# Attention of a two-layer kernel: four PSUM banks for scores and three for maxima, maxima ordered beside scores of the other half, heads written out

## The chip, the core and the metric

One core of a Trainium2 chip runs the whole program. The metric is the time of one execution on the device in microseconds; lower is better. Three runs of the kernel before give the median that the change is measured against.

## What is computed

Two layers, each a gated cross-attention and a gated mixture-of-experts feed-forward on x of 2048 x 256. The keys and values of both layers come from the same context of 1601 x 256. There are 16 heads of depth 16. The change touches the attention alone:

```python
q = split(layernorm(x) @ wq.T + bq); k = split(ctx @ wk.T + bk); v = split(ctx @ wv.T + bv)
scores = einsum('bhqd,bhkd->bhqk', q, k) / sqrt(16)
scores = where(mask == 0, -inf, scores)          # layer 0 only
p = softmax(scores); x = x + tanh(g) * (einsum('bhqk,bhkd->bhqd', p, v) @ wo.T + bo)
# routed feed-forwards follow each attention: one expert of 8 in layer 0, two of 8 in layer 1
```

Layer 0's mask leaves keys only in a stretch at the end of the context. If they fit a window of 512 keys, which they do here, `attend` runs over that window (4 key tiles); layer 1 runs over all 1601 keys (13 key tiles, the last of 65 keys).

## The kernel before

`attend` (L589 on) computes all 16 heads of one layer. TensorE, ScalarE and VectorE each have an instruction list of their own, written in the order in which they are to run, tied by counting semaphores (`wait`). An engine stands at a wait until its semaphore is high enough, and all that is behind in its list stands too.

Each head needs two passes over its scores. The first finds the maxima of the rows: TensorE computes scores with queries as rows (`entry`, L798: one *piece* is 128 queries x 400 keys, 16 x 4 = 64 pieces a head in layer 1; 128 x 512, 16 pieces, in layer 0) and VectorE reduces each to a column (`piece`, L910). When all are done VectorE reduces again to `row_max` (L944), TensorE transposes it (`maxima`, L787), VectorE splits it into two parts (`split_max`, L916, L918), and a DMA puts them into rows of the queries' operand. The second pass computes scores with keys as rows (`scores`, L809: 128 keys x 512 queries, four *columns* S0 to S3 a key tile), less the maximum by those rows; ScalarE takes the exponential into `probs` (L890), and `times_values` (PV, L826) multiplies with the values, four matmuls side by side into one bank, `o_bank`. A further column of ones gives the sums. After the last key tile ScalarE copies `o_bank` out (`copy_out`, L873), TensorE transposes it (`sums`, L791), and VectorE takes the reciprocal and multiplies (`norm`, L926, L929).

The two passes are interleaved: iteration i makes the maxima of head i, and the exponentials and products of heads i-1 and i-2. An iteration has KT *steps* (13 in layer 1, 4 in layer 0), and each step takes its share of pieces (`cuts`): five in twelve steps of layer 1 and four in the first; four in each step of layer 0. A step s < `late` (4, or 2 in layer 0) works at the last key tiles of head i-2, the others at head i-1. The transpose of the maxima stands in step 1 of layer 1 (step 0 of layer 0) as the third entry; the sums stand at the end of step 6 (3). Both count as two entries. Iterations 16 and 17 only drain: they have no pieces.

TensorE's list in a step with pieces p0 to p4 is: S0, S1, p0, p1, S2, p2, PV, S3, p3, p4. PV is for the key tile of the step before. The scores of even columns and the pieces of even number use rows 0 to 63 of the array, the others rows 64 to 127; two matmuls on different halves can run side by side.

Banks and waits: the scores go round three banks of PSUM, and a score waits for the exponential of the third score before it. The entries (pieces, transposes) go round four banks (`BANKS`), and entry n waits for VectorE to be done with entry n-4 (`entry_done`). `o_bank` takes the eighth bank. PV waits for all four exponentials of its key tile.

The iterations run through `iterations`: 0 to 3 are written out, 4 to 15 are a loop in the engines' instructions whose body has three iterations (so three jumps back), 16 and 17 are written out. In the loop, waits compare with values held in registers. SP, which issues the loads of the next head's keys and queries, has a loop of its own.

Of the kernel before, what the change touches and what calls it, by code (L numbers as in the profile page):

```python
# [22 lines left out]
F32 = mybir.dt.float32  # L23
# [3 lines left out]
ALU = mybir.AluOpType  # L27
ACT = mybir.ActivationFunctionType
# [23 lines left out]
BANKS = 4  # L52
# [327 lines left out]
class Keys:  # L380


    def __init__(self, first, size, pieces, late, maxima_at):
        self.first, self.S, self.pieces = first, size, pieces
        self.KT = -(-size // P)
        self.late = late
        self.maxima_at = maxima_at
        self.sums_at = min(late + 2, self.KT - 1)
        assert sum(n for _, n in pieces) == size and (NC * self.KT) % RING == 1
# [199 lines left out]
def attend(nc, const, scratch, l, keys, attn, row_max, mask=None, key_mask=None):  # L589
# [9 lines left out]
    with ExitStack() as ctx:  # L599
# [12 lines left out]
        s_bank = [sc.ps(f"s_bank{n}", [P, CH], F32) for n in range(RING)]  # L612
# [27 lines left out]
        assert ENTRIES % BANKS == 0 and (NC * KT) % RING == 1  # L640

        def entries(mx, tail, fresh):


            steps, n = [], 0
            for s in range(KT):
                now = list(range(cuts[s], cuts[s + 1])) if mx else []
                if fresh and s == keys.maxima_at[0]:
                    now.insert(keys.maxima_at[1] if mx else 0, "maxima")
                now += ["sums"] * (s == keys.sums_at and tail)  # L650
                steps.append([])
                for what in now:
                    n += places(what)
                    steps[-1].append((what, n - 1))
            return steps, n
# [20 lines left out]
        def bank_of(i, n):  # L676
            return p_bank[((entries_before(i) if isinstance(i, int) else -6) + n) % BANKS]

# [4 lines left out]
        def iterations(eng, body):  # L683

            def once(i):
                body(i, i % RING, i < H, i >= 2, 1 <= i <= H)
            for i in range(4):
                once(i)
            with eng.Fori(4, H - RING + 1, RING) as j:
                for u in range(RING):  # L690
                    body(j + u, (4 + u) % RING, True, True, True)
            for i in range(H, H + 2):
                once(i)
# [14 lines left out]
        def _(sp):  # L708
# [43 lines left out]
            with sp.Fori(4, H - RING, RING) as j:  # L752
                for u in range(RING):
                    body(j + u, (4 + u) % RING, True, True, True)
            for i in range(H - RING, H + 1):
                body(i, i % RING, True, True, True)
# [21 lines left out]
        def _(pe):  # L778
# [3 lines left out]
            def entry(i, slot, what, n):  # L782
                wait(pe, entry_done, entries_before(i) + (n - BANKS + 1))
                bank = bank_of(i, n)
                if what == "maxima":
                    wait(pe, max_ready, i)
                    last = pe.transpose(bank[0:QT, 0:P], row_max[:, (slot - 1) % RING, :], const["ident"][:, :])  # L787
                elif what == "sums":
                    wait(pe, o_copied, i - 1)
                    for b in range(NC):  # L790
                        last = pe.transpose(bank[:, b * P:(b + 1) * P], o_sb[:, b * P:(b + 1) * P],  # L791
                                            const["ident"][:, :])
                else:
                    t, c = tile_of(what)
                    k0, kn = PIECES[c]
                    a, t = divmod(t, QT // 2)
                    rows = slice(a * SIDE, a * SIDE + ROWS)
                    last = pe.matmul(bank[:, 0:even(kn)], q_st[rows, slot, t * P:(t + 1) * P].bitcast(F32R),  # L798
                                     k_st[rows, slot, k0:k0 + even(kn)].bitcast(F32R), start=True, stop=True)
                last.then_inc(entry_ready, places(what))  # L800

            def scores(h, hs, kt, c):
                kn, q0 = keys_of(kt), chunk_of(c)
                if not isinstance(h, int) or NC * (KT * h + kt) + c >= RING:
                    wait(pe, exp_done, h * (NC * KT) + (NC * kt + c - RING + 1), apart=masked)
                out = s_bank[(NC * kt + c + hs) % RING][0:kn, :]
# [24 lines left out]
            def body(i, slot, mx, tail, fresh):  # L831
# [6 lines left out]
                for s in range(KT):  # L838
# [3 lines left out]
                    for chunks, first, end in (((0, 1), 0, 2), ((2,), 2, 3), ((3,), 3, None)):  # L842
# [10 lines left out]
        def _(act):  # L853
# [21 lines left out]
            def body(i, slot, mx, tail, fresh):  # L875
                for s in range(KT):
# [3 lines left out]
                    if now:  # L880
# [4 lines left out]
                        for c in range(NC):  # L885
                            if c == NC - 1 and s == LATE and tail:
# [4 lines left out]
                                           s_bank[(NC * kt + c + hs) % RING][0:kn, :], ACT.Exp).then_inc(exp_done, 1)  # L891
# [4 lines left out]
        def _(dve):  # L896
# [3 lines left out]
            def piece(i, slot, what, n):  # L900
# [4 lines left out]
                if masked:  # L905
                    dve.tensor_tensor_reduce(junk[:, n % BANKS, 0:kn], bank_of(i, n)[:, 0:kn],
                                             mask[:, t, k0:k0 + kn], 1.0, -3.0e38, ALU.add, ALU.max, dst)\
                        .then_inc(entry_done, 1)
                else:
                    dve.tensor_reduce(dst, bank_of(i, n)[:, 0:kn], AX.X, ALU.max).then_inc(entry_done, 1)  # L910

            def split_max(i, n):

                wait(dve, entry_ready, entries_before(i) + (n + 1))
                turned = bank_of(i, n)[0:QT, 0:P]
# [6 lines left out]
            def norm(i, slot, n):  # L922

                wait(dve, entry_ready, entries_before(i) + (n + 1))
                sums = bank_of(i, n)[:, :].rearrange("p (b c v) -> p b c v", b=NC, v=VW)
# [6 lines left out]
            def body(i, slot, mx, tail, fresh):  # L932
                listed, many = entries(mx, tail, fresh)
                for step in listed:
                    for what, n in step:
                        if what == "maxima":
                            split_max(i, n)
# [882 lines left out]
def flamingo_kernel(nc, io, out):  # L1820
# [10 lines left out]
    with ExitStack() as ctx:  # L1831
# [16 lines left out]
        everything = Keys(0, S, PIECES, 4, (1, 2))  # L1848
        for l in range(2):
            if l:  # L1850
                clear_semaphores(nc)
            with ExitStack() as part:
# [17 lines left out]
                else:  # L1870
                    attend(nc, const, scratch, l, everything, attn, row_max)
# [48 lines left out]
```

## Time and profile before

| | |
|---|---|
| median of 3 runs | 1890.03 us (1886.89 to 1894.4) |
| profiled execution | 1891.61 us, its span 1889.9 us |
| mean granted TensorE clock | 0.901 |
| PE busy | 1545.9 us (82%) |
| DVE busy | 1178.3 us (62%) |
| ACT busy | 861.1 us (46%) |
| POOL busy | 182.0 us (10%) |
| attention of layer 0 | first piece at 169.7 us, last norm at 385.5 us |
| attention of layer 1 | last norm at 1585.5 us; row maxima of its heads from 967.0 to 1537.2 us |

PE is TensorE's matmuls, DVE VectorE, ACT ScalarE, POOL GpSimd, SP the engine that issues DMAs. A row of a timeline has the start in us from the span's start, the time that it covers, the engine, the line of the kernel, what is written and read, and how many instructions were merged (x3). In square brackets stands how long the engine had been idle and what ended that. The ends of matmuls are modelled, and some records can be missing, so starts are the better numbers. In the table of windows the columns are: from and to, length, busy time (and count) of PE, PE's weight loads, DVE, ACT and POOL, then TensorE's granted clock as a share of full speed, the DMA engines' busy share and GB/s. The windows of rows 2 run from one row maximum (L944) to a later one, that is over whole heads: one head, three heads, three single heads, 13 heads of layer 0, and a part of the drain.

### The profile page before, as it was taken

The page shows a single profiled execution, that of the slowest core. Times are in us where ns is not written, and L with a number is a line of the kernel's source. Part 1 is how long each engine was busy: PE and PEld are TensorE (multiplying, and loading weights), DVE is VectorE, ACT ScalarE, POOL GpSimd, SP SyncE. Part 2 cuts the span into 40 slices and gives each one's busy share as a digit, 9 for nine tenths or more (in the row PEclk, how much of TensorE's full clock was granted, in tenths as well). Part 3 has the DMA queues.
Part 4 walks back from the last instruction along what each step waited for, and adds up shares of the span by engine and source line. Part 5 has one row for each costly group of instructions (what it writes and reads, how often), then busy time and mean ns, then how long its engine had stood idle before and what let it go on. Part 6 is the DMA issues. An engine that isn't in the chain of part 4 may idle for free. (4 is left out here: it accounts for less than half of the span.)

```text
span 1889.9 us, 27747 instructions
## 1 busy us (share of the span) xinstructions
PE 1545.9 (82%) x7833; PEld 910.5 (48%) x7834; DVE 1178.3 (62%) x2309; ACT 861.1 (46%) x1544; POOL 182.0 (10%) x248
## 2 busy tenths in 40 slices
PE   6464999968997999992399999999999998657880
PEld 3132443347785788882154444444444434544550
DVE  2564988763211677766398888888898853622334
ACT  3021767722112555541127777676776775221110
POOL 3520000000300000003000000000000000061106
PEclk9786999987999999996659999999999999788995
DMA  7935312111102899971722121111211100424114
GB/s 242 373 116 156 102 43 51 27 46 67 45 1 88 300 348 336 335 250 48 212 67 67 42 44 23 22 22 30 35 22 22 22 1 1 113 89 129 38 50 133
DMA packets 108654, 196.61 MB, mean 104 GB/s; under 512 B 8958, under 2 KB 80371, under 8 KB 108567
## 3 DMA queue, kind: packets, MB, share of 16 engines
q1 hardware_dynamic: 101633, 180.71, 30.9%
q0 software_dynamic: 4608, 12.59, 2.1%
q10 hardware_dynamic: 2326, 2.31, 0.4%
q8 instruction: 36, 0.59, 0.1%
q14 instruction: 51, 0.42, 0.1%
HBM read 144.69 MB, written 50.36 MB: 103 GB/s over the span
## 5 line engine op out<-in xcount | busy, mean ns | idle before, releaser
L910 DVE TENSOR_REDUCE attend_piece_max<-attend_p_bank 128x1 f32<-128x400 f32 (+3 forms) x1280 | 671.8, 588 | 108.1 <-PE attend_p_bank L798 90.7
L890 ACT ACTIVATE attend_probs<-attend_s_bank 128x512 f32<-128x512 f32 (+1 forms) x1088 | 565.3, 602 | 284.4 <-PE attend_s_bank L809 284.2
L798 PE MATMUL attend_p_bank<-attend_k_st,attend_q_st 62*128 62x400 f32 (+2 forms) x1280 | 412.3, 418 | 62.8 <-DMA attend_k_st<-ones_rows 52.3
L809 PE MATMUL attend_s_bank<-attend_q_st,attend_k_st 64*128 64x512 f32 (+1 forms) x1088 | 385.5, 461 | 26.8 <-ACT attend_probs L890 13.6
L809 PEld LDWEIGHTS attend_s_bank<-attend_q_st,attend_k_st 64*128 64x128 f32 (+1 forms) x1088 | 170.9, 185 | 348.9 <-ACT attend_probs L890 338.0
L826 PE MATMUL attend_o_bank<-attend_probs,attend_v_st 128*32 128x512 f32 (+1 forms) x2176 | 293.4, 611 | 1.4 <-ACT attend_probs L890 1.4
L798 PEld LDWEIGHTS attend_p_bank<-attend_k_st,attend_q_st 62*128 62x128 f32 x1280 | 223.1, 198 | 109.5 <-issue 54.0
L1520 DVE TENSOR_TENSOR slots_w_low<-slots_w_up,slots_w_high 128x2048 fp32r<-128x2048 f32 x46 | 105.1, 2287 | 46.9 <-ACT slots_w_high L1516 46.9
L1330 DVE TENSOR_TENSOR share_hid<-share_b_bank,share_g_act 128x512 f32<-128x512 f32 (+1 forms) x40 | 27.6, 691 | 120.5 <-PE share_b_bank L1181 89.8
L1516 ACT ACTIVATE slots_w_high<-slots_w_up 128x2048 fp32r<-128x2048 f32 x46 | 87.8, 1910 | 6.8 <-DMA slots_w_up<-in_L_ffn_W_dram 6.6
L1787 POOL DMA_INDIRECT collect_back<-back,keep_f_place x48 | 47.0, 980 | 386.4 <-PEq L1776 372.4
L1476 PE MATMUL slots_y_bank<-slots_w_dn,slots_hid_t 128*128 128x256 f32 x368 | 83.2, 379 | 1.0 <-DVE slots_hid_t L1527 1.0
L773 POOL COPY attend_v_st<-attend_values 128x64 f32 (+3 forms) x32 | 9.3, 298 | 735.7 <-PE attend_o_bank L826 706.5
L1148 POOL DMA_INDIRECT sorted<-keep_x_x_n,keep_f_place x48 | 48.3, 1005 | 324.9 <-DVE keep_f_place L1313 310.9
L1757 DVE TENSOR_TENSOR slots_hid<-slots_u_bank,slots_g_act 128x192 f32<-128x192 f32 x39 | 13.9, 358 | 101.9 <-ACT slots_g_act L1743 101.9
L826 PEld LDWEIGHTS attend_o_bank<-attend_probs,attend_v_st 128*32 128x32 f32 (+1 forms) x2176 | 42.9, 108 | 69.8 <-ACT attend_probs L890 47.9
L1193 PE MATMUL share_y_bank<-share_w_dn,share_hid 128*128 128x256 f32 (+1 forms) x320 | 71.2, 382 | 6.1 <-DVE share_hid L1330 6.1
L1690 PE MATMUL slots_u_bank<-keep_f_up,slots_x_t 128*128 x156 | 63.3, 530 | 14.8 <-issue 12.9
L1476 PEld LDWEIGHTS slots_y_bank<-slots_w_dn,slots_hid_t 128*128 128x128 f32 x368 | 69.7, 190 | 11.3 <-issue 1.2
L1193 PEld LDWEIGHTS share_y_bank<-share_w_dn,share_hid 128*128 128x128 f32 (+1 forms) x320 | 60.0, 190 | 17.1 <-DVE share_hid L1330 9.1
L1218 ACT ACTIVATE share_g_act<-share_a_bank 128x512 f32<-128x512 f32 (+1 forms) x40 | 23.9, 598 | 83.5 <-PE share_a_bank L1181 72.2
L1743 ACT ACTIVATE slots_g_act<-slots_u_bank 128x192 f32<-128x192 f32 x39 | 12.9, 330 | 102.0 <-PE slots_u_bank L1690 102.0
(234 smaller groups left out, 1811.0 us busy)
## 6 DMA issues: line engine op xcount, KB each, us to landing
slots_w_up<-in_L_ffn_W_dram SPq DMA_DIRECT2D x46, 1024.0 KB, 7.9
slots_w_dn<-in_L_ffn_W_dram SPq DMA_DIRECT2D x23, 1024.0 KB, 6.1
ctx_raw<-in_mask_BxSxS_ik_dram SPq DMA_DIRECT2D x16, 800.5 KB, 8.1
q_rows<-q_part SPq DMA_DIRECT2D x24, 512.0 KB, 4.3
attend_q_st<-q_rows SPq DMA_DIRECT2D x64, 192.0 KB, 4.6
k_rows<-ctx_k_part SPq DMA_DIRECT2D x12, 800.5 KB, 10.5
attend_k_st<-k_rows SPq DMA_DIRECT2D x32, 300.2 KB, 6.1
sorted<-keep_zeros SPq DMA_DIRECT2D x6, 1024.0 KB, 8.5
```

Of the source, the lines that this page charges most:

```text
L798: last = pe.matmul(bank[:, 0:even(kn)], q_st[rows, slot, t * P:(t + 1) * P].bitcast(F32R), k_st[rows, slot, k0:k0 + even(kn)].bitcast(F32R ...
L809: last = pe.matmul(out, k_st[rows, hs, kt * P:kt * P + kn].bitcast(F32R), q_st[rows, hs, q0:q0 + CH].bitcast(F32R), start=True, stop=not m ...
L826: last = pe.matmul(o_bank[c * VW:(c + 1) * VW, :], v_st[0:kn, hs, kt, :], probs[0:kn, (kt + hs) % RING, c * CH:(c + 1) * CH], start=(kt == ...
L890: act.activation(probs[0:kn, (kt + hs) % RING, q0:q0 + CH], s_bank[(NC * kt + c + hs) % RING][0:kn, :], ACT.Exp).then_inc(exp_done, 1)
L910: dve.tensor_reduce(dst, bank_of(i, n)[:, 0:kn], AX.X, ALU.max).then_inc(entry_done, 1)
L1148: pool.indirect_dma_start(scratch["sorted"][l][:, :], bass.IndirectOffsetOnAxis(ap=place[:, k, t:t + 1], axis=0), x_n[:, t], None).then_in ...
L1193: last = pe.matmul(y_bank[n % 2][:, :], hid[:, c % 2, f, t * P:(t + 1) * P], w_dn[:, f], start=(f == 0), stop=(f == FT - 1))
L1476: last = pe.matmul(y_bank[:, 0:D], hid_t[:, slot, f], w_dn[:, slot, f], start=(f == 0), stop=(f == FT - 1))
L1516: act.activation(w_high[:, half].bitcast(F32R), loaded(slot, half), ACT.Copy).then_inc(w_rounded, 1)
L1520: dve.tensor_tensor(w_low[:, half].bitcast(F32R), loaded(slot, half), w_high[:, half], ALU.subtract)\
L1690: last = pe.matmul(u_bank[k][:, 0:2 * F], x_t[:, k, b], resident["up"][:, e, b].rearrange("p a n f -> p (a n f)"), start=(b == 0), stop=(b ...
L1787: pool.indirect_dma_start(back[:, k, t], None, scratch["back"][l][:, :], bass.IndirectOffsetOnAxis(ap=place[:, k, t:t + 1], axis=0))\
```

## The change

1. Four score banks (one for each column), three banks for entries. A score now waits for the exponential of the same column of the key tile before; entry n waits for entry n-3. As 68 entries a head don't divide by three, the bank depends on the iteration's slot.
2. `side_by_side` reorders the pieces of a step, so that the first is of the other half than S0, the second of the other half than S1, and so on. TensorE's list becomes S0, p0, S1, p1, S2, p2, PV, S3, p3, p4.
3. With `looped=False` all heads are written out, without a loop in the instructions, on each engine. Layer 1 and layer 0's window run so; only the branch of layer 0 that isn't taken here keeps the loop.

```diff
-BANKS = 4
+BANKS = 3
...
-        s_bank = [sc.ps(f"s_bank{n}", [P, CH], F32) for n in range(RING)]
+        s_bank = [sc.ps(f"s_bank{n}", [P, CH], F32) for n in range(NC)]
         p_bank = [sc.ps(f"p_bank{n}", [P, CH], F32) for n in range(BANKS)]
...
+        def side_by_side(now):
+
+            halves, taken = [now[1::2], now[0::2]] if now and now[0] % 2 == 0 else [now[0::2], now[1::2]], []
+            for k in range(len(now)):
+                taken.append((halves[k % 2] or halves[1 - k % 2]).pop(0))
+            return taken
...
-                now = list(range(cuts[s], cuts[s + 1])) if mx else []
+                now = side_by_side(list(range(cuts[s], cuts[s + 1]))) if mx else []
...
-        def bank_of(i, n):
-            return p_bank[((entries_before(i) if isinstance(i, int) else -6) + n) % BANKS]
+        def bank_of(i, slot, n):
+            return p_bank[((entries_before(i) if isinstance(i, int) else slot * ENTRIES - 6) + n) % BANKS]
...
-            for i in range(4):
+            for i in range(4 if keys.looped else H):
                 once(i)
-            with eng.Fori(4, H - RING + 1, RING) as j:
-                for u in range(RING):
-                    body(j + u, (4 + u) % RING, True, True, True)
+            if keys.looped:
+                with eng.Fori(4, H - RING + 1, RING) as j:
+                    for u in range(RING):
+                        body(j + u, (4 + u) % RING, True, True, True)
...
-            with sp.Fori(4, H - RING, RING) as j:
-                for u in range(RING):
-                    body(j + u, (4 + u) % RING, True, True, True)
-            for i in range(H - RING, H + 1):
+            if keys.looped:
+                with sp.Fori(4, H - RING, RING) as j:
+                    for u in range(RING):
+                        body(j + u, (4 + u) % RING, True, True, True)
+            for i in range(H - RING if keys.looped else 4, H + 1):
                 body(i, i % RING, True, True, True)
...
             def scores(h, hs, kt, c):
                 kn, q0 = keys_of(kt), chunk_of(c)
-                if not isinstance(h, int) or NC * (KT * h + kt) + c >= RING:
-                    wait(pe, exp_done, h * (NC * KT) + (NC * kt + c - RING + 1), apart=masked)
-                out = s_bank[(NC * kt + c + hs) % RING][0:kn, :]
+                if not isinstance(h, int) or KT * h + kt > 0:
+                    wait(pe, exp_done, h * (NC * KT) + (NC * kt + c - NC + 1), apart=masked)
+                out = s_bank[c][0:kn, :]
...
-                    for chunks, first, end in (((0, 1), 0, 2), ((2,), 2, 3), ((3,), 3, None)):
+                    for chunks, first, end in (((0,), 0, 1), ((1,), 1, 2), ((2,), 2, 3), ((3,), 3, None)):
                         if chunks == (3,) and before:
                             times_values(*before)
...
-        everything = Keys(0, S, PIECES, 4, (1, 2))
+        everything = Keys(0, S, PIECES, 4, (1, 2), looped=True)
+        unmasked = Keys(0, S, PIECES, 4, (1, 2))
...
-                    attend(nc, const, scratch, l, everything, attn, row_max)
+                    attend(nc, const, scratch, l, unmasked, attn, row_max)
```

## Rows read from the trace of the kernel before

**Rows 1.** Page, costliest groups: busy us, mean ns, idle before, releaser.

```profile
L910 DVE TENSOR_REDUCE attend_piece_max<-attend_p_bank 128x1 f32<-128x400 f32 (+3 forms) x1280 | 671.8, 588 | 108.1 <-PE attend_p_bank L798 90.7
```

**Rows 2.** Windows: length, busy us and count by engine, clock, DMA.

```profile
1040.14:1077.69 37.55, 35.86 (x227) 15.73 (x225) 33.26 (x70) 27.50 (x54) 0.36 (x1) 1.00 0.24 53
...
1077.69:1189.64 111.95, 107.71 (x677) 47.40 (x675) 99.97 (x207) 82.19 (x160) 1.08 (x3) 1.00 0.17 29
...
1189.64:1230.43 40.79, 37.37 (x227) 16.71 (x225) 33.27 (x69) 27.66 (x54) 0.36 (x1) 0.96 0.14 26
...
1305.12:1347.06 41.94, 38.61 (x227) 17.35 (x225) 33.27 (x70) 27.73 (x54) 0.36 (x1) 0.92 0.14 25
...
1421.71:1462.53 40.82, 37.34 (x227) 16.68 (x225) 33.27 (x69) 27.64 (x54) 0.36 (x1) 0.96 0.15 26
...
203.46:366.21 162.75, 155.40 (x895) 65.29 (x894) 144.82 (x273) 115.24 (x222) 2.84 (x12) 1.00 0.19 45
...
1556.94:1577.74 20.80, 17.19 (x97) 5.09 (x96) 0.00 (x0) 16.52 (x34) 0.00 (x0) 1.00 0.00 1
```

**Rows 3.** Timeline of TensorE, a step of layer 1: start, us, instruction.

```profile
1135.56 0.45 PE L798 MATMUL attend_p_bank<-attend_k_st,attend_q_st 62*128 62x400 f32 x1 [0.21 <-DVE keep_a_attn L929]
...
1135.93 1.07 PE L826 MATMUL attend_o_bank<-attend_probs,attend_v_st 128*32 128x512 f32 x8
...
1136.93 0.49 PE L809 MATMUL attend_s_bank<-attend_q_st,attend_k_st 64*128 64x512 f32 x1
...
1138.11 0.50 PE L809 MATMUL attend_s_bank<-attend_q_st,attend_k_st 64*128 64x512 f32 x1
...
1138.28 0.44 PE L798 MATMUL attend_p_bank<-attend_k_st,attend_q_st 62*128 62x402 f32 x1
...
1138.65 0.64 PE L826 MATMUL attend_o_bank<-attend_probs,attend_v_st 128*32 128x512 f32 x4
```

**Rows 4.** The same stretch, VectorE.

```profile
1135.08 0.42 DVE L929 TENSOR_TENSOR keep_a_attn<-attend_p_bank,attend_inv_sum 128x256 f32 x1 [0.20 <-DVE attend_inv_sum L926]
...
1135.42 1.52 DVE L910 TENSOR_REDUCE attend_piece_max<-attend_p_bank 128x1 f32<-128x400 f32 x3
...
1137.65 1.53 DVE L910 TENSOR_REDUCE attend_piece_max<-attend_p_bank 128x1 f32<-128x400 f32 x3 [0.70 <-PE attend_p_bank L798]
```

**Rows 5.** The same stretch, ScalarE.

```profile
1137.46 2.06 ACT L890 ACTIVATE attend_probs<-attend_s_bank 128x512 f32<-128x512 f32 x4 [1.07 <-PE attend_s_bank L809]
```

**Rows 6.** Timeline around the maxima's transpose, layer 1.

```profile
1117.76 0.28 PE L787 MATMUL attend_p_bank<-keep_ident,keep_a_row_max 128*16 128x128 f32 x1
...
1117.96 1.06 PE L826 MATMUL attend_o_bank<-attend_probs,attend_v_st 128*32 128x512 f32 x8
...
1118.96 0.50 PE L809 MATMUL attend_s_bank<-attend_q_st,attend_k_st 64*128 64x512 f32 x1
...
1119.53 2.50 DVE L910 TENSOR_REDUCE attend_piece_max<-attend_p_bank 128x1 f32<-128x399 f32 x5 [0.56 <-PE attend_p_bank L798]
...
1121.01 1.06 PE L826 MATMUL attend_o_bank<-attend_probs,attend_v_st 128*32 128x512 f32 x8
```

**Rows 7.** Timeline of layer 1's drain, where no maxima are made.

```profile
1562.14 1.06 PE L826 MATMUL attend_o_bank<-attend_probs,attend_v_st 128*32 128x512 f32 x8
...
1563.14 0.73 PE L809 MATMUL attend_s_bank<-attend_q_st,attend_k_st 64*128 64x512 f32 x3
...
1563.67 1.57 ACT L890 ACTIVATE attend_probs<-attend_s_bank 128x512 f32<-128x512 f32 x3 [0.54 <-PE attend_s_bank L809]
...
1564.32 0.49 PE L809 MATMUL attend_s_bank<-attend_q_st,attend_k_st 64*128 64x512 f32 x1 [0.45 <-ACT attend_probs L890]
...
1564.74 0.64 PE L826 MATMUL attend_o_bank<-attend_probs,attend_v_st 128*32 128x512 f32 x4
```

**Rows 8.** Timeline of TensorE in layer 1's fill, low clock.

```profile
979.53 1.93 PE L826 MATMUL attend_o_bank<-attend_probs,attend_v_st 128*32 128x512 f32 x8
...
983.82 0.64 PE L826 MATMUL attend_o_bank<-attend_probs,attend_v_st 128*32 128x512 f32 x4
```

More of the change, by code:

```diff
@@ L380, with __init__ @@
 class Keys:
-    def __init__(self, first, size, pieces, late, maxima_at):
+    def __init__(self, first, size, pieces, late, maxima_at, looped=False):
+        self.looped = looped
         self.first, self.S, self.pieces = first, size, pieces
@@ L639, in attend @@
         ENTRIES = PER + 4
-        assert ENTRIES % BANKS == 0 and (NC * KT) % RING == 1
+        assert (NC * KT) % RING == 1 and BANKS == RING
+        def side_by_side(now):
[3 more added lines that the diff above has]
+            return taken
         def entries(mx, tail, fresh):
@@ L783, in entry @@
                 wait(pe, entry_done, entries_before(i) + (n - BANKS + 1))
-                bank = bank_of(i, n)
+                bank = bank_of(i, slot, n)
                 if what == "maxima":
@@ L890, in body @@
                             act.activation(probs[0:kn, (kt + hs) % RING, q0:q0 + CH],
-                                           s_bank[(NC * kt + c + hs) % RING][0:kn, :], ACT.Exp).then_inc(exp_done, 1)
+                                           s_bank[c][0:kn, :], ACT.Exp).then_inc(exp_done, 1)
             iterations(act, body)
@@ L905, in piece @@
                 if masked:
-                    dve.tensor_tensor_reduce(junk[:, n % BANKS, 0:kn], bank_of(i, n)[:, 0:kn],
+                    dve.tensor_tensor_reduce(junk[:, n % BANKS, 0:kn], bank_of(i, slot, n)[:, 0:kn],
                                              mask[:, t, k0:k0 + kn], 1.0, -3.0e38, ALU.add, ALU.max, dst)\
@@ L909, in piece, with split_max @@
                 else:
-                    dve.tensor_reduce(dst, bank_of(i, n)[:, 0:kn], AX.X, ALU.max).then_inc(entry_done, 1)
-            def split_max(i, n):
+                    dve.tensor_reduce(dst, bank_of(i, slot, n)[:, 0:kn], AX.X, ALU.max).then_inc(entry_done, 1)
+            def split_max(i, slot, n):
                 wait(dve, entry_ready, entries_before(i) + (n + 1))
-                turned = bank_of(i, n)[0:QT, 0:P]
+                turned = bank_of(i, slot, n)[0:QT, 0:P]
                 dve.tensor_scalar(m_part[:, 0].bitcast(F32R), turned, -1.0, None, ALU.mult).then_inc(max_high, 1)
@@ L924, in norm @@
                 wait(dve, entry_ready, entries_before(i) + (n + 1))
-                sums = bank_of(i, n)[:, :].rearrange("p (b c v) -> p b c v", b=NC, v=VW)
+                sums = bank_of(i, slot, n)[:, :].rearrange("p (b c v) -> p b c v", b=NC, v=VW)
                 dve.reciprocal(inv_sum[:, slot], sums[:, :, :, DK]).then_inc(inverted, 1)
@@ L936, in body @@
                         if what == "maxima":
-                            split_max(i, n)
+                            split_max(i, slot, n)
                         elif what == "sums":
```

## The prediction

> **What bounds the kernel now.** I read the costliest groups of the page first. The costliest one, the maxima's reductions on VectorE (L910, 671.8 us), lies in the two attention stages [rows 1], and so does the change. The windows then show two things. A head of layer 1 takes 111.95 / 3 = 37.32 us (the time from one head's row maximum to the next), of which VectorE works 99.97 / 3 = 33.3 us; a head of layer 0 takes 162.75 / 13 = 12.52 us with 144.82 / 13 = 11.14 us of VectorE [rows 2]. So VectorE is nearest to being full, yet idle 11% of each head. And in layer 1 three heads take 40.79, 41.94 and 40.82 us instead of 37.32: each holds a jump back of the hand-written loop over three heads [rows 2].
>
> The timeline says why VectorE idles. A step is one tile of 128 keys: four score matmuls S0 to S3, five maxima matmuls p0 to p4 and PV, the values matmul. In one step PV starts at 1138.65, after S at 1138.11 and p at 1138.28; the step before, PV starts at 1135.93 and S3 at 1136.93 behind it [rows 3]. ScalarE's four exponentials start at 1137.46 [rows 5], 0.53 after S3. S2 of the next step wants the bank of this first exponential (three score banks), so it starts at 1138.11. That makes a ring: S3, 0.53, exponential 0.60, release 0.05, S2 to PV 0.54, PV to S3 1.00, together 2.72 us, the distance 1135.93 to 1138.65 exactly [rows 3, 5]. (Where p2 uses the same half of the array as S2, it can't run beside it, and the ring is about 0.07 longer; steps alternate between 2.72 and 2.79, mean 2.76.) The drain, where no maxima are made, shows the ring bare: S3 1563.14, exponential 1563.67, S2 1564.32, PV 1564.74, against PV 1562.14 before: 2.60 us [rows 7]. VectorE needs only 5 x 0.48 = 2.4 us in a step (three reductions in 1.52, the last 0.56 long [rows 4]), and then waits for the p behind PV (0.70 us in the row shown, after the sums [rows 4]; in a regular step 2.76 - 4 x 0.48 - 0.56 = 0.26 on average).
>
> **Four score banks.** S2 now needs the exponential of its own column in the step before, which is long past. PV still needs the exponential that follows S3. Without maxima the ring is 0.53 + 0.60 + 0.05 + 1.00 = 2.18 instead of 2.60: 0.42 less [rows 7]. Some 15 such steps in layer 1's drain and 5 in layer 0's give -6.3 and -2.1 us.
>
> **Three maxima banks.** Entry n waits for the reduction of n-3, not n-4, and TensorE takes its instructions in order. The entry just ahead of PV is p2. In a five-piece step the entries before it are p1, p0, and then p4 of the step before. So p2, and PV queued behind it, now wait until p4 has been reduced; with four banks it was p3, one reduction earlier. How this reads on the trace: VectorE ends norm at 1135.08 + 0.42 = 1135.50, the p that waits for it starts at 1135.56, PV at 1135.93, S3 at 1136.93 [rows 3, 4]. So: release 0.06, lone p to PV 0.37, PV to S3 1.00. From an S3 with its p beside it to the reduction it takes 0.57 (1118.96 to 1119.53 [rows 6]); where p shares the half it is 0.72 (1136.93 to 1137.65 [rows 3, 4]). The new ring is: p3's reduction starts 0.57 after S3, p4's 0.48 later, it takes 0.56, release 0.06, p2 to PV 0.37, PV to S3 1.00: 3.04 us against 2.76, +0.28 a step. Low bound: if PV followed p2 by 0.30 (0.17 of its columns and little else) 2.97; and if p4 were reduced where it is now relative to ScalarE, no less than 2.72. High bound: p3 not beside S3, 0.15 more, 3.19. I take 3.04, since each piece has a row.
>
> **The order of maxima.** p0 to p3 get the other half from S0 to S3. That keeps p3 at 0.57 in every step (now in every second), and is in the 3.04 already; it also makes S2 and p2 cheap, but S2 is no longer on the path, so this is worth nothing. In the step with the maxima transpose the order slips by one: the p behind S3 falls on S3's half, 0.15 later.
>
> **One head of layer 1.** Ten of 13 steps are rings of 3.04: +2.8 us. The transpose's step: it waits for p0 (one reduction after p3) and PV is 0.20 behind it (1117.76 to 1117.96 [rows 6]): 1.57 + 0.48 + 0.56 + 0.06 + 0.20 = 2.87, +0.1. The step after: 1.00 + 0.72 + 2 x 0.48 + 0.99 = 3.67, where 1121.01 - 1117.96 = 3.05 stands now [rows 6], +0.6. The step after the sums: they take two places in the ring of banks, so p1 and p2 both wait for norm, where now only p2 does: +0.20 for p1, +0.17 since p2 no longer stands alone, and the transposes start one release later, about +0.35: +0.7. Head: 37.3 + 4.2 = 41.5. For the 14 full heads +58.4; the first head with scores has eight or so such steps, +2.2.
>
> **One head of layer 0** has four steps of four pieces of 512 columns, and this p2 waits for p3 of the step before: 0.61 + 0.68 + 0.06 + 0.40 + 1.00 = 2.75 (an estimate: the terms above with 112 more columns, 0.04 of TensorE and 0.12 of VectorE). Two steps are such. The one after the transpose has p2 on S3's half and two reductions behind it: 1.00 + 0.76 + 0.61 + 0.68 + 0.06 + 0.40 = 3.5. In the step after the sums norm starts some 2.7 after PV, p0's reduction 0.57 behind it, and the transpose waits for that one: 2.7 + 0.57 + 0.68 + 0.06 + 0.20 = 4.2. Head 2 x 2.75 + 3.5 + 4.2 = 13.2 against 12.52, 14 heads: +9.5.
>
> **Heads written out.** The three jumps back cost 3.5 + 4.6 + 3.5 = 11.6 us of layer 1, with TensorE's clock down to 0.92 to 0.96 in those heads; they go [rows 2]. Layer 0's heads differ by 0.1 at most with a jump: -0.4. What the longer code costs: heads 2 and 3 are written out already, and one of them takes 37.55 against 37.32 [rows 2]. Bounds: between nothing and 0.23 x 12 = 2.8; I take nothing, for its DMA share is also the higher (0.24 against 0.17: the zeros being stored). Each engine, SP with its loads too, keeps its order; register arithmetic for waits leaves the sequencers and is on no path, since the rings above close without it. On the cause the Trainium skill has a rule (Runtime: NRT & Kernel Launch, "Instruction fetch mechanics"): a taken branch whose target is out of the fetch window waits for a fetch, straight code is fetched ahead. By that rule the 11.6 us go whole, and the trace agrees on the jumps' place.
>
> **Sum**, against the profiled execution's own 1891.6: layer 1 +58.4 + 2.2 - 11.6 - 6.3; layer 0 +9.5 - 0.4 - 2.1: +49.7, 1941.3. The median of the three runs is 1.6 lower than the profiled one: 1939.7.
>
> **Rivals.**
> - *The gate of p2 holds less than I say* (slower by half): p4 reduced earlier, or PV closer to p2, ring 2.90, half of the attention's +70: 1905. It is inside my range. For it: the ring has six terms of 0.05 to 1.0, each modelled in the records.
> - *Steps keep 2.76* because p4's reduction never ends after the exponential: only jumps and drain count, 1890.0 - 20.4 = 1870. Against it: p3's reduction starts 0.57 after S3 and the exponential 0.53, both 0.6 long; p4's ends 0.5 later. Chance 0.06.
> - *VectorE becomes the bound and full*, what the fourth score bank could give with maxima banks to spare: heads 33.3 and 11.1, 14 x 4.0 + 14 x 1.4 = 76 less, and 20 more: 1794. Against it: with three banks VectorE has 3 x 0.48 = 1.45 us of stock from p2's start, and PV, S3 and p3 take 0.37 + 1.00 + 0.57 = 1.94. Chance 0.06.
> - *TensorE's clock falls.* The new step holds some 0.5 us in which TensorE waits for p2. At the low level a step took 983.82 - 979.53 = 4.29 us [rows 8]; if half the steps of the 14 heads ran so, 91 x 1.2 = 109 more: 2049. Against it: the drain waits in every 2.60 us step (S2 at 1564.32 behind a wait [rows 7]) and the full level is granted there: 1.00 from 1556.94 to 1577.74 [rows 2]. Chance 0.04. The Trainium skill's page TensorE: Matmul & The Clock Gate ("A second HAM failure mode: psum-queue depth-cycling") speaks for this rival: short idles between groups that cycle PSUM banks made another kernel's clock oscillate. The row of the drain doesn't show it.
>
> **How the numbers follow.** Forecast and the half case together 0.84: nearly all of it more than 0.5% (9.5 us) above 1890, which is what a measurement of this kernel can tell from no change. Faster 0.12 by the second and third rival, same 0.03, slower 0.85. The range runs from the half case, 1905, to the unpaired ring (0.15 x 13 x 14 = 27, of which I take 20): 1960. It leaves out the two faster rivals and the clock, 0.16, and a little of the rest.
>
> **What would show it.** Right: row maxima of layer 1 some 41.5 us apart, of layer 0 13.2; PV to PV 3.04 in a regular step; the p ahead of PV released by L910 of VectorE and starting 0.06 after a reduction's end; VectorE's idle time before p3 near 3.04 - 4 x 0.48 - 0.56 = 0.54 us instead of 0.26; no head of 41 to 42 among heads of another length; PV to PV 2.2 in the drain. Wrong: PV released by L890, or PV to PV at or under 2.76 in layer 1; a clock under 1.00 in the regular heads would be the last rival.

## The result, and the profile after

The changed kernel takes 1937.84 us (median of 4 runs, 1935.05 to 1940.19) against 1888.85 for the kernel before beside it: 1.025 times, 95% interval 1.021 to 1.029. Forecast were 1939.7 and 1905 to 1960. The profiled execution spans 1938.5 us, 48.6 more than before. (Here and below, the ratios and intervals leave out a run at a markedly lower clock and over 1.5% above the kernel's fastest, one of e2's four; the medians hold all runs.)

On the page, the idle time ahead of the reductions has grown (162.8 us; 108.1 in rows 1), and so has that of TensorE's weight loads (PEld) ahead of the maxima, most of it ended by VectorE. The third line is the one of before:

```profile
L920 DVE TENSOR_REDUCE attend_piece_max<-attend_p_bank 128x1 f32<-128x400 f32 (+3 forms) x1280 | 674.6, 591 | 162.8 <-PE attend_p_bank L808 161.7
...
L808 PEld LDWEIGHTS attend_p_bank<-attend_k_st,attend_q_st 62*128 62x128 f32 x1280 | 211.3, 195 | 257.3 <-DVE attend_piece_max L920 183.7
...
L798 PEld LDWEIGHTS attend_p_bank<-attend_k_st,attend_q_st 62*128 62x128 f32 x1280 | 223.1, 198 | 109.5 <-issue 54.0
```

The windows of the changed kernel, with the columns of rows 2: 14 full heads of layer 1, a regular head of it, two heads that were longer, 13 heads of layer 0, and a part of the drain.

```profile
1008.71:1591.78 583.07, 529.99 (x3156) 225.20 (x3156) 469.12 (x966) 387.26 (x743) 4.68 (x13) 0.99 0.15 29
...
1050.09:1091.48 41.39, 37.62 (x226) 15.99 (x225) 33.51 (x69) 27.64 (x54) 0.36 (x1) 1.00 0.22 48
...
1257.04:1299.79 42.75, 38.98 (x226) 16.50 (x225) 33.51 (x69) 27.74 (x54) 0.36 (x1) 0.96 0.14 25
...
1465.33:1508.99 43.66, 40.10 (x227) 17.04 (x225) 33.48 (x69) 27.92 (x54) 0.36 (x1) 0.92 0.14 25
...
194.70:364.50 169.80, 160.43 (x895) 64.71 (x895) 145.08 (x273) 117.91 (x222) 3.07 (x13) 1.00 0.22 54
...
1604.90:1626.70 21.80, 19.36 (x122) 6.19 (x120) 0.42 (x1) 20.45 (x41) 0.00 (x0) 1.00 0.00 1
```

A regular head of layer 1 takes 41.39 us where rows 2 have 37.32, one of layer 0 169.80 / 13 = 13.06 where they have 12.52. VectorE works in a head what it did (33.51 and 33.3): it only waits longer. Two heads have 42.75 and 43.66: they hold no jump; TensorE's clock fell to the low level in them (mean 0.96 and 0.92), both times in the step behind PV of the tile of 65 keys, 2.2 to 2.3 us after that PV started. In the step where it fell, the next PV covers 1.93 us instead of 1.06:

```profile
1273.38 1.93 PE L836 MATMUL attend_o_bank<-attend_probs,attend_v_st 128*32 128x512 f32 x8
```

```profile
1481.70 1.93 PE L836 MATMUL attend_o_bank<-attend_probs,attend_v_st 128*32 128x512 f32 x8
```

One regular step of TensorE, VectorE and ScalarE, to be laid beside rows 3 to 5. Of the scores, the first of these lines is S3 and the second S2 of the next step; of the maxima, p1 and p2 are shown:

```profile
1200.79 1.06 PE L836 MATMUL attend_o_bank<-attend_probs,attend_v_st 128*32 128x512 f32 x8
...
1201.79 0.50 PE L819 MATMUL attend_s_bank<-attend_q_st,attend_k_st 64*128 64x512 f32 x1
...
1202.50 0.39 PE L819 MATMUL attend_s_bank<-attend_q_st,attend_k_st 64*128 64x512 f32 x1
...
1202.99 0.45 PE L808 MATMUL attend_p_bank<-attend_k_st,attend_q_st 62*128 62x400 f32 x1
...
1203.47 0.45 PE L808 MATMUL attend_p_bank<-attend_k_st,attend_q_st 62*128 62x400 f32 x1
...
1203.84 1.06 PE L836 MATMUL attend_o_bank<-attend_probs,attend_v_st 128*32 128x512 f32 x8
```

```profile
1202.36 2.50 DVE L920 TENSOR_REDUCE attend_piece_max<-attend_p_bank 128x1 f32<-128x400 f32 x5 [0.55 <-PE attend_p_bank L808]
```

```profile
1202.32 2.06 ACT L900 ACTIVATE attend_probs<-attend_s_bank 128x512 f32<-128x512 f32 x4 [0.98 <-PE attend_s_bank L819]
```

PV starts at 1200.79, S3 at 1201.79 and the next PV at 1203.84, so the step takes 3.05 us. The exponential of S3 (1202.32 to 1202.92) has ended 0.92 before PV starts, so it holds nobody. p1 and p2 come at 1202.99 and 1203.47. The reductions start at 1202.36 and then each 0.48 later, and the last is 0.56 long. So the one of p3 ends at about 1202.92 and the one of p4 at 1203.41: each p starts 0.06 to 0.07 behind one. PV follows p2 by 0.37. VectorE idles 0.55 before p3's reduction. The waits of the weight loads over the 14 heads say the same, the changed kernel first:

```profile
PEld attend_s_bank L819 <- ACT attend_probs L900: 151.5, 180, 1.4
...
PEld attend_p_bank L808 <- DVE attend_piece_max L920: 124.2, 318, 0.9
```

```profile
PEld attend_s_bank L809 <- ACT attend_probs L890: 223.2, 343, 0.8
...
PEld attend_p_bank L798 <- DVE attend_piece_max L910: 18.0, 45, 2.1
```

The wait for the exponentials has shrunk from 223 to 152 us, and the wait for the reductions has grown from 18 us in 45 places to 124 us in 318. In the drain PV follows PV by 2.18 us (2.60 in rows 7):

```profile
1609.28 1.07 PE L836 MATMUL attend_o_bank<-attend_probs,attend_v_st 128*32 128x512 f32 x8 [0.22 <-ACT attend_probs L900]
...
1611.46 1.07 PE L836 MATMUL attend_o_bank<-attend_probs,attend_v_st 128*32 128x512 f32 x8 [0.22 <-ACT attend_probs L900]
...
1613.64 0.64 PE L836 MATMUL attend_o_bank<-attend_probs,attend_v_st 128*32 128x512 f32 x4 [0.22 <-ACT attend_probs L900]
```

### The profile page after: what moved, and what is told of

It reads as the page before. It is cut to its first block and busy times, and to the rows that moved or that the text cites. A ratio compares the mean times of both kernels' runs of the same rounds, so it can differ in the third digit from the quotient of the medians.

```text
span 1938.5 us, 23827 instructions
## 1 busy us (share of the span) xinstructions
PE 1569.8 (81%) x7833; PEld 911.9 (47%) x7834; DVE 1182.4 (61%) x2309; ACT 866.9 (45%) x1544; POOL 183.1 (9%) x248
## 5 line engine op out<-in xcount | busy, mean ns | idle before, releaser
L920 DVE TENSOR_REDUCE attend_piece_max<-attend_p_bank 128x1 f32<-128x400 f32 (+3 forms) x1280 | 674.6, 591 | 162.8 <-PE attend_p_bank L808 161.7
L900 ACT ACTIVATE attend_probs<-attend_s_bank 128x512 f32<-128x512 f32 (+1 forms) x1088 | 571.7, 601 | 327.1 <-PE attend_s_bank L819 324.0
L808 PE MATMUL attend_p_bank<-attend_k_st,attend_q_st 62*128 62x400 f32 (+2 forms) x1280 | 459.8, 446 | 97.5 <-DMA attend_k_st<-ones_rows 50.2
L819 PE MATMUL attend_s_bank<-attend_q_st,attend_k_st 64*128 64x512 f32 (+1 forms) x1088 | 375.2, 429 | 0.0
L808 PEld LDWEIGHTS attend_p_bank<-attend_k_st,attend_q_st 62*128 62x128 f32 x1280 | 211.3, 195 | 257.3 <-DVE attend_piece_max L920 183.7
L783 POOL COPY attend_v_st<-attend_values 128x64 f32<-128x64 f32 (+1 forms) x32 | 9.3, 298 | 788.0 <-PE attend_o_bank L836 760.9
L1158 POOL DMA_INDIRECT sorted<-keep_x_x_n,keep_f_place x48 | 48.5, 1011 | 320.6 <-DVE keep_f_place L1323 306.6
```

The source lines that it names most:

```text
L819: last = pe.matmul(out, k_st[rows, hs, kt * P:kt * P + kn].bitcast(F32R), q_st[rows, hs, q0:q0 + CH].bitcast(F32R), start=True, stop=not m ...
L900: act.activation(probs[0:kn, (kt + hs) % RING, q0:q0 + CH], s_bank[c][0:kn, :], ACT.Exp).then_inc(exp_done, 1)
L920: dve.tensor_reduce(dst, bank_of(i, slot, n)[:, 0:kn], AX.X, ALU.max).then_inc(entry_done, 1)
L1158: pool.indirect_dma_start(scratch["sorted"][l][:, :], bass.IndirectOffsetOnAxis(ap=place[:, k, t:t + 1], axis=0), x_n[:, t], None).then_in ...
```

## The experiments

Two theories stand against each other in most of them. The *gate*: the entry ahead of PV waits for the reduction as many entries back as there are banks, PV is queued behind it, and VectorE runs dry while PV holds TensorE. The *rivals*: the written-out code, the new order, or the fourth score bank is what costs. Lengths of steps are distances from PV to PV in the traces. The diffs are cut to what matters ("...").

**Loops put back (e1_looped).**

```diff
-        unmasked = Keys(0, S, PIECES, 4, (1, 2))
+        unmasked = Keys(0, S, PIECES, 4, (1, 2), looped=True)
...
-        keys = Keys(start, WINDOW, [(0, WINDOW)], 2, (0, 2))
+        keys = Keys(start, WINDOW, [(0, WINDOW)], 2, (0, 2), looped=True)
```

> The changed kernel with the loop over three heads put back in both layers; banks and order as changed. Gate theory (p2 waits for the reduction three entries back, PV is queued behind it): PV to PV stays at 3.05 us in a regular step, the three jumps back return in layer 1 with 11.6 us: 1938 + 11 = 1949. Rival (written-out code is what costs): the regular step falls under 2.9 and the time under 1925.

Measured: 1960.2 us, 1.036 times the kernel before (1.028 to 1.043). Regular steps keep 3.05 us, so the written-out code isn't what costs. But the loop costs 22 us here, not 11: the 14 heads take 605.33 us at a mean clock of 0.96, where they take 583.07 at 0.99 written out. The heads with a jump have 48.5, 47.8 and 47.8 us at clocks of 0.86 to 0.89. The step with the jump is about 2.7 us longer than the same step elsewhere (2.5 in the kernel before); most of the rest is the low clock. Three heads without a jump hold a fall of the clock too.

```profile
1015.25:1620.58 605.33, 547.48 (x3156) 233.11 (x3156) 469.05 (x966) 388.69 (x744) 4.69 (x13) 0.96 0.14 28
```

**Before, written out (e2_written).** Only `Fori` is dropped from the kernel before, as in the change.

> The kernel before with its heads written out, nothing else. Gate theory: the regular steps stay at 2.72 and 2.79 us, the heads of 41 to 42 us go: 1889 - 12 = 1877. Rival (written-out code costs): 1889 or more.

Measured: 1871.64 us, 0.989 (0.979 to 0.998); one of the four runs took 1900.24 at a mean clock of 0.88. No head is longer than 37.2. The 14 heads take 520.16 us against 534.20:

```profile
995.94:1516.10 520.16, 501.72 (x3153) 219.70 (x3155) 465.93 (x967) 383.79 (x743) 4.71 (x13) 1.00 0.16 32
```

11.6 us of these 14.0 are the heads with a jump. The other 2.4 are spread over the heads, 37.16 for 37.33, and layer 0's went from 12.52 to 12.32 too. One piece of it is seen at norm. In rows 4, from the loop, VectorE idles 0.20 us between the reciprocal and norm; in e2 it is 0.36 - 0.25 = 0.11:

```profile
1126.91 0.25 DVE L929 RECIPROCAL attend_inv_sum<-attend_p_bank 128x16 f32<-128x16 f32 x1
...
1127.27 0.42 DVE L932 TENSOR_TENSOR keep_a_attn<-attend_p_bank,attend_inv_sum 128x256 f32<-128x256 f32 x1
```

At this place the loop has two things that written-out heads lack: a wait for a value in a register, and a no-op behind it (`apart` in `wait`). No run parts the two. The trace of before shows the gain already: its written-out head 2 takes 37.15 us and idles 0.10 at norm, and layer 0's written-out heads 2 and 3 take 12.32 each. Head 3 of layer 1, also written out, takes 37.55 because it idles 0.47 there, once, just ahead of the loop; e1 has the same wait there, e2 has none.

**Three score banks and four entry banks, new order, written out (e3_s3p4).**

```diff
-BANKS = 3
+BANKS = 4
...
-        s_bank = [... for n in range(NC)]
+        s_bank = [... for n in range(RING)]
...
-                    wait(pe, exp_done, h * (NC * KT) + (NC * kt + c - NC + 1), apart=masked)
-                out = s_bank[c][0:kn, :]
+                    wait(pe, exp_done, h * (NC * KT) + (NC * kt + c - RING + 1), apart=masked)
+                out = s_bank[(NC * kt + c + hs) % RING][0:kn, :]
```

> The changed kernel with three score banks and four entry banks again; new order of the maxima and written-out heads stay. Gate theory: PV to PV 2.72 in every regular step, since S2 and p2 are always on different halves (before: 2.72 and 2.79 by turns); drain 2.60; some 5 us under e2, about 1872. Rival (the order is what costs, as p0 now stands between S0 and S1): PV to PV over 2.8 and the time over 1890.

Measured: 1840.34 us, 0.973 (0.966 to 0.980). The sign is the gate's, the size is not: 31 us under e2 where 5 were expected, with regular steps of 2.60 and 2.61 instead of 2.72. In the traces 18.8 us of it are in the 14 heads of layer 1 and 8.1 in those of layer 0. Another 6.6 are not the order's: in e2's drain, which holds no maxima, the clock fell (mean 0.83), and in e3's it did not. A regular step of TensorE:

```profile
1123.86 1.07 PE L836 MATMUL attend_o_bank<-attend_probs,attend_v_st 128*32 128x512 f32 x8
...
1124.86 0.50 PE L819 MATMUL attend_s_bank<-attend_q_st,attend_k_st 64*128 64x512 f32 x1
...
1126.04 0.50 PE L819 MATMUL attend_s_bank<-attend_q_st,attend_k_st 64*128 64x512 f32 x1
...
1126.06 0.45 PE L808 MATMUL attend_p_bank<-attend_k_st,attend_q_st 62*128 62x400 f32 x1
...
1126.47 1.07 PE L836 MATMUL attend_o_bank<-attend_probs,attend_v_st 128*32 128x512 f32 x8
```

S2 and p2 start together (1126.04, 1126.06), one when the exponential is done, the other when p3's reduction is, and PV follows S2 by 0.43. In rows 3 the same stretch takes 0.54: there p3 shared the half with S3 and was reduced 0.15 later, so p2 came 0.17 after S2. The order pays by bringing two gates that open at almost the same time to the same moment, on two halves.

**Three and three (e4_s3p3).** The score banks of e3, entry banks as changed.

> The changed kernel with three score banks and three entry banks (one bank unused), so only the entry banks differ from e3 and only the score banks from the changed kernel. Gate theory: the step is that of the entry banks, 3.05 us, and only the drain goes back from 2.18 to 2.60: 1938 + 8 = 1946. Rival (the fourth score bank is what slows the steps, since scores crowd in ahead of p2): steps at 2.75 and about 1875.

Measured: 1947.95 us, 1.031 (1.023 to 1.038). Steps take 3.05 us, those of the drain 2.60. Between e3 and e4 stands one bank for entries: 108 us. Between e4 and the changed kernel stands one for scores: 10 us, of which the two drains are 8.2 in the traces (6.7 and 1.5). The 14 heads are 581.52 us here, with one fall of the clock, and 583.07 in the changed kernel, with two, so between the drains the fourth score bank is worth nothing.

**PV ahead of p2 (e5_pv_early).**

```diff
-                    for chunks, first, end in (((0,), 0, 1), ((1,), 1, 2), ((2,), 2, 3), ((3,), 3, None)):
+                    for chunks, first, end in (((0,), 0, 1), ((1,), 1, 2), ((2,), 2, 2), ((3,), 2, None)):
```

> The changed kernel with PV one place earlier: S0, p0, S1, p1, S2, PV, S3, p2, p3, p4. Now p1 stands ahead of PV and waits for p3's reduction, one earlier; but VectorE also starts one piece earlier on what comes behind PV. Gate theory: what counts is how many filled banks VectorE has while PV holds TensorE, not which piece stands ahead of PV; p2 is on S3's half, so the ring is 0.72 + 0.48 + 0.56 + 0.06 + 0.37 + 1.00 = 3.19: about 1960. Rival (it is p2's place ahead of PV): the ring falls to 2.6 to 2.7, about 1885.

Measured: 2107.7 us (one run). At the full clock a step takes 3.44 us:

```profile
1242.18 1.07 PE L836 MATMUL attend_o_bank<-attend_probs,attend_v_st 128*32 128x512 f32 x8
...
1243.17 0.50 PE L819 MATMUL attend_s_bank<-attend_q_st,attend_k_st 64*128 64x512 f32 x1
...
1245.01 0.45 PE L808 MATMUL attend_p_bank<-attend_k_st,attend_q_st 62*128 62x400 f32 x1
...
1245.30 0.39 PE L819 MATMUL attend_s_bank<-attend_q_st,attend_k_st 64*128 64x512 f32 x1
...
1245.61 0.64 PE L836 MATMUL attend_o_bank<-attend_probs,attend_v_st 128*32 128x512 f32 x4
```

p1 waits (1245.01), S2 stands behind it on its half (1245.30), PV behind both: 0.60 from p1 to PV instead of the 0.37 in my sum, which had forgotten S2. 3.19 + 0.23 = 3.42. So PV doesn't run sooner when p2 is behind it, and the ring closes with the term put right. Of the 170 us over the changed kernel, some 95 are the longer steps by an estimate: at the full clock this kernel's heads would take about 46.4 us in layer 1 (41.4 in the changed kernel), from its own full-clock steps, and 14.8 in layer 0 (13.1). Most of the other 75 is the clock: over a quarter of the 14 heads ran at the low level, with steps of 5.19.

```profile
1044.49:1761.17 716.68, 631.28 (x3159) 261.98 (x3158) 470.49 (x966) 407.56 (x744) 4.69 (x13) 0.86 0.12 24
```

**Two entry banks (e6_p2).** `BANKS = 2` in the changed kernel.

> The changed kernel with two entry banks instead of three. Gate theory: p2 waits for p0's reduction of the same step, and p0 for p3's: ring 0.57 + 1.07 + 0.56 + 0.06 + 0.37 + 1.00 = 3.63 us a regular step, a head of layer 1 some 49 us; with layer 0 and the fill about 2090. Rival (the banks of the maxima are not what holds PV): steps stay near 3.05, under 1960.

Measured: 2371.15 us (one run), far over the 2090 expected. At the full clock a regular step takes 3.68 us (PV 1194.42 to 1198.10), 0.05 over the 3.63 worked out, but two thirds of the time the clock is low and a step takes 5.35. The 14 heads here, and for comparison those of e3:

```profile
1139.82:2026.34 886.52, 811.55 (x3158) 324.31 (x3158) 501.29 (x966) 409.40 (x743) 4.69 (x13) 0.67 0.10 19
```

```profile
985.88:1487.23 501.35, 478.23 (x3152) 199.31 (x3155) 464.63 (x967) 384.83 (x743) 4.71 (x13) 1.00 0.17 34
```

**PV last (e7_s3p4_pv_last), on both allotments (e8_s4p3_pv_last), and with the last pair exchanged (e11_pv_last_pair).**

```diff
-                    for chunks, first, end in (((0,), 0, 1), ((1,), 1, 2), ((2,), 2, 3), ((3,), 3, None)):
-                        if chunks == (3,) and before:
-                            times_values(*before)
...
+                    at3 = 4 if NP > 1 else 3
+                    for c, first, end in ((0, 0, 1), (1, 1, 2), (2, 2, at3), (3, at3, None)):
...
+                    if before:
+                        times_values(*before)
```

This is the edit of e7 and e8; e11 has it too, and exchanges two maxima in `side_by_side`:

```diff
+            if taken and taken[-1] % 2 == 1:
+                taken[-2:] = taken[:-3:-1]
```

> e3 (three score banks, four entry banks, written out) with PV last in the step: S0, p0, S1, p1, S2, p2, p3, S3, p4, PV. S3 no longer stands behind PV, so the exponential that PV waits for is a step old. Gate theory: two rings are left, S0 to exponential 0.53 + 0.60 + 0.05 to S3, 0.4 to PV, 1.00 to the next S0 = 2.58; and VectorE, whose four banks hold 4 x 0.48 = 1.94 us against 0.37 + 1.00 + 0.57 = 1.94, so 2.42 to 2.5. PV to PV 2.5 to 2.6 in layer 1: 1835 to 1850. Rival (something else, TensorE's own work say, sets 2.7): no less than 1870.

Measured: 1903.15 us (ten runs), 1.005 (1.001 to 1.009). A miss: 50 to 70 us over the expectation. The ten runs lie in two groups: four from 1884.8 to 1889.4 at a mean clock of 0.901 to 0.905, six from 1902.3 to 1907.7 at 0.890 to 0.892. The trace is one of the second. Its steps alternate between 2.66 and 2.86:

```profile
1136.00 0.50 PE L819 MATMUL attend_s_bank<-attend_q_st,attend_k_st 64*128 64x512 f32 x1
...
1136.33 0.34 PE L808 MATMUL attend_p_bank<-attend_k_st,attend_q_st 62*128 62x400 f32 x1
...
1136.60 1.06 PE L836 MATMUL attend_o_bank<-attend_probs,attend_v_st 128*32 128x512 f32 x8
...
1138.84 0.49 PE L819 MATMUL attend_s_bank<-attend_q_st,attend_k_st 64*128 64x512 f32 x1
...
1138.85 0.45 PE L808 MATMUL attend_p_bank<-attend_k_st,attend_q_st 62*128 62x400 f32 x1
...
1139.26 0.64 PE L836 MATMUL attend_o_bank<-attend_probs,attend_v_st 128*32 128x512 f32 x4
```

In one step S3 (1136.00) and the p behind it (1136.33) are on one half and PV comes 0.60 after S3; in the next (1138.84, 1138.85, 1139.26) 0.42. The step with the transpose grew to 3.62 (2.81 in e3) and the one behind the tile of 65 keys to 3.19 (2.70). From its sixth step on, the drain ran at the low clock with steps of 4.12; it took 63.8 us, against 44.1 in e3. That alone is of the size of the gap between the two groups of runs.

> The same order as e7 on the changed kernel's banks, four for scores and three for entries. Gate theory: VectorE's stock is 1.45 us against 1.94, so the step is 2.42 + 0.5 to 0.6 = 3.0 whatever the order: 1930 to 1945. Rival (the order makes e7's gain, the banks don't matter): as e7.

Measured: 1936.26 us (one run), steps of 3.05. With three entry banks PV last gives the same regular step as PV ahead of S3; PV earlier still (e5) gives a longer one.

> e7 (PV last, three score and four entry banks) with the last two maxima exchanged where the last is on S3's half, so that S3 and the piece behind it always run side by side. e7's steps alternate between 2.66 and 2.86 us, and the trace has 0.42 from S3 to PV in the one and 0.60 in the other. If that half is the cause: 2.66 in every regular step of layer 1, heads of 37.0 instead of 38.0, some 14 us less than e7's 1903. If not: steps of 2.66 and 2.86 as before.

Measured: 1877.8 us (one run). All regular steps take 2.66 or 2.67: the half was the cause of the longer ones. The 14 heads take 11.5 us less than e7's; most of the rest of the 25 us under e7's median is e7's drain (47.2 us here). 2.66 is still over e3's 2.60, and the steps of 3.62 and 3.19 stay, so this order gives less than e3's. Although its steps are short, four of its heads hold a fall of the clock:

```profile
997.63:1522.87 525.24, 482.16 (x3153) 201.77 (x3149) 465.99 (x966) 382.42 (x742) 4.70 (x13) 0.99 0.17 32
```

**Old order on the changed banks (e9_old_order).** `side_by_side` out, groups of S and p as before.

> The changed kernel with its four and three banks and written-out heads, but with the order of before: S0, S1, p0, p1, S2, p2, PV, S3, p3, p4, pieces in their plain order. Gate theory, as in the prediction (the order is worth only p3's place beside S3): PV to PV alternates between 3.05 and 3.20 in layer 1, and is 2.89 instead of 2.74 in layer 0; about 12 us more than the changed kernel, 1950. Rival (with three entry banks too the order gives what it gave from e2 to e3, 31 us): about 1969 and steps of 3.2 throughout.

Measured: 1955.33 us, 1.036 (1.032 to 1.039). Steps of 3.05 and 3.20 by turns, 2.93 in layer 0, heads of 42.15 and 13.46 instead of 41.39 and 13.07: (0.76 + 0.39) x 14 = 16. Two heads had a fall of the clock, as many as in the changed kernel, one of them a longer one (48.75). In the heads of both layers the order is worth 16 us on the changed banks, all of it in the steps in which p3 lost its place beside S3 or its like in layer 0, and 27 us with four entry banks (e3 against e2).

**The step with the transpose paired too (e10_s3p4_max).**

```diff
                     now.insert(keys.maxima_at[1] if mx else 0, "maxima")
+                    if mx:
+                        now[3], now[4] = now[4], now[3]
```

> e3 (three score banks, four entry banks, new order, written out) with two pieces exchanged in the step that has the maxima's transpose, so that the piece behind S3 is on the other half there too. If the pairing behind S3 is worth 0.15 us wherever VectorE waits for that piece: the step after the transpose 3.20 to 3.05 in layer 1, 2.93 to 2.79 in layer 0, 4 us in all: 1836. If VectorE is busy with the split of the maxima until then anyway: no change from 1840.

Measured: 1838.28 us, 0.974 (0.971 to 0.977). The step goes from 3.20 to 3.05 in layer 1 and from 2.93 to 2.73 in layer 0, in every head of the trace; the difference from e3 in time, 2 us, is within the spread of the runs.

## Why the prediction was right

- *The present ring, and its release.* Right. Rows 7's drain went from 2.60 to 2.18 us, as worked out. In layer 1 it gave 8.2 us (row maximum of the last head to the last PV, 45.2 and 37.0), where 6.3 were forecast. Some 1.5 of it are a fall of the clock that the drain of before held: e4, with three score banks and no such fall, is 6.7 longer than the changed kernel there.
- *The gate of p2.* Right, to the size: 3.04 forecast, 3.05 measured, and by the releaser named. That the fourth bank for scores doesn't matter between the drains is shown by e4, and that PV behind S3 changes nothing by e8; that the number of entry banks does matter, by e3 (four: 2.60), e4 and the change (three: 3.05) and e6 (two: 3.68).
- *The head.* 41.5 forecast, 41.39 measured: the transpose's step 2.92 (2.87), the one after it 3.67 (3.67), the one after the sums 4.34 (about 4.55). Layer 0: 13.2 and 13.06.
- *The order.* Right for this kernel (p3's place, e9: 16 us in the heads), but "worth nothing" for S2 and p2 holds only with three entry banks. The 0.54 from S2 to PV was not a constant of the matmuls: 0.11 of it was p2's own wait, which four banks had left too. e3 shows that.
- *Written out.* The jumps were sized right (11.6 us, e2). That the loop's register arithmetic "is on no path" can't be right as it stands, for the loop costs more than its jumps: e2 has 0.17 to 0.20 us a head less in each layer, some 5 us; whether that is register arithmetic or the no-ops that go with it stays open. The bounds of 0 to 0.23 us more a head for longer code had the wrong sign: they took one written-out head, 37.55, and not the other, 37.15. The rule of the Trainium skill (Runtime: NRT & Kernel Launch, "Instruction fetch mechanics") fits: the jumps' stall is gone in e2 and in the changed kernel, and no stall of its kind is seen in the longer code.
- *The clock.* The rival came true in a small part: two heads, 1.4 and 2.3 us. The evidence against it was read too kindly: the window of the drain at 1.00 begins just behind a fall in the same drain.

```profile
1547.00:1558.00 11.00, 10.00 (x51) 3.23 (x51) 0.68 (x2) 8.19 (x16) 0.00 (x0) 0.84 0.00 1
```

For e5 and e6 I gave the clock no part. By the steps at the full clock it is under half of e5's loss and some 180 of the 303 us that e6's 14 heads lose (an estimate, from a full-clock head of about 50 us).
- *The sum.* Over the two attentions' parts the traces give +48.9 (14 heads of layer 1, 583.07 - 534.20) against 46.8, +2.4 (first head) against 2.2, -8.2 against -6.3, and in layer 0 +7.8 and -1.6 against 9.1 and -2.1: +49.3 against 49.7. That the whole comes within 2 us is partly luck, for this list leaves out four moves that the prediction had not forecast. The first head of layer 0 took 1.6 us more (12.55 and 11.00; 12.46 to 12.74 in e1, e4 and e9, with three entry banks too). The stretch ahead of the attention took 2.0 more, the one behind layer 1's last PV 2.2 more, and the one between the attentions 6.5 less (545.7 and 552.3 us from layer 0's last PV to layer 1's first piece). That last stretch lies between 543.8 and 548.4 in all the other traces, looped ones too, so it is the trace of before that stands out; why stays open.

The bank that was moved did what it was moved for only where there are no maxima. Elsewhere the step was held by two rings of nearly equal length, and the bank was taken from the ring of entries, which needed it, and given to the ring of scores. The changed kernel's order and written-out heads are worth 48 us, and the exchange of the banks costs 98 (e3 and the changed kernel). e10 has the former without the latter: 1838.3 us, 0.974 of the kernel before.

## What to carry to other kernels

Before a buffer is moved from one ring to another, work out the length of both rings that pass through the blocking instruction: the stock that n buffers hold (n times the consumer's pace) against the time in which the producer is away. Here four banks hold 4 x 0.485 = 1.94 us of reductions, and from p2's start to the next reduction pass 1.94 (to PV 0.37, to S3 1.00, to the reduction 0.57): just covered. Three banks don't cover it; the 0.485 that is missing is nearly the whole growth of the step from 2.60 to 3.05. Where two gates open at nearly the same time, align them and put what they release on different halves of the array: that was worth 27 us in the heads here.

## What had not been expected of the hardware

The clock's loss grows far faster than the waits. The kernels compared here do the same work in TensorE in a head. With steps of 2.60 us the mean clock over the 14 heads was 1.00 (e3), with 3.05 it was 0.99 (the change), with 3.44 it was 0.86 (e5), with 3.68 it was 0.67 (e6). At the low level (1.2 GHz, where the granted clock reads 0.50) the step took 5.19 and 5.35 us. e6's TensorE, busy in 811.55 of 886.52 us by the (modelled) records, went on at it for up to 61 us.

But the step's mean length is not what decides. e7 and e11, with steps of 2.66 to 2.86, had three and four heads with a fall, and e4, with 3.05, had one. What these falls share is their place: in the changed kernel, e4, e7, e8, e9 and e11 all 14 of them begin 2.2 to 2.7 us after the start of the PV of the tile of 65 keys, which has 65 rows instead of 128, and the fall in the drain of before begins 3.0 us after one. Whether the 65 rows are the cause no run tests; e2, e3 and e10 have the same tile and no fall in these heads. The Trainium skill (TensorE: Matmul & The Clock Gate, "A second HAM failure mode: psum-queue depth-cycling") tells of such an oscillation where TensorE idles shortly between groups of matmuls. e5 and e6 agree with it; e7 and e11 show that some falls come with shorter waits as well.
